# Two LoRA layers on one core: earlier loads of x and of layer 1's rows, and three slots instead of two for transposed x

## The reference, cut to what matters

```python
# layer 0 (adapters 6..15 of 32 are named by the ids), layer 1 (3..7 of 8)
x = x + (einsum('bsd,od->bso', x, base_weight) + base_bias
         + einsum('bsr,bor->bso', einsum('bsd,brd->bsr', x, lora_A_w[ids0]), lora_B_w[ids0]))
x = x + einsum('bnr,bor->bno', einsum('bni,bri->bnr', x, B[ids1]), A[ids1])   # SCALING is 1
```

## Time and profile before

| | us |
|---|---|
| median of 3 runs | 98.22 (97.95 to 98.42) |
| the profiled execution | 97.92 |
| its span, first to last instruction | 95.8 |
| PE busy | 91.5 (96%) |
| DVE, ACT, POOL busy | 64.8, 58.7, 58.0 |

### The profile page before, as it was taken

How to read it: one execution, slowest core, us unless ns; L and a number is a source line. 1 busy time by engine, 2 the same in 40 slices (tenths; PEclk the granted TensorE clock), 3 DMA queues, 4 the chain that set the end, 5 groups by cost and what they waited for, 6 DMA issues and landing times.

```text
span 95.8 us, 2305 instructions
## 1 busy us (share of the span) xinstructions
PE 91.5 (96%) x662; PEld 90.0 (94%) x662; DVE 64.8 (68%) x120; ACT 58.7 (61%) x189; POOL 58.0 (61%) x126
## 2 busy tenths in 40 slices
PE   5999999999999999999999999999999999999980
PEld 5899999999899998999999999999999999999970
DVE  4499799227076468959587877768595868786460
ACT  0074598874588796748494948567584949480210
POOL 6504008850568999999576584959585766808500
PEclk9999999999999999999999999999999999999998
DMA  2999998968896289989996499992836354520205
GB/s 40 312 347 387 374 403 262 281 156 214 215 224 223 53 250 238 310 249 235 203 290 218 70 319 209 238 269 91 228 44 229 34 213 54 200 110 0 110 0 219
DMA packets 16335, 19.45 MB, mean 203 GB/s; under 512 B 1444, under 2 KB 11556, under 8 KB 16164
## 3 DMA queue, kind: packets, MB, share of 16 engines
q1 hardware_dynamic: 15040, 14.04, 50.1%
q0 software_dynamic: 1280, 5.28, 22.1%
q10 hardware_dynamic: 4, 0.00, 0.0%
HBM read 13.47 MB, written 5.84 MB: 202 GB/s over the span
## 4 chain that ended last, share of the span: by engine, by line
PE 90%; DVE 4%; ACT 2%; issue 1%; DVEq 0%; ACTq 0%
PE psum L394 55%; PE psum L440 11%; PE psum L432 4%; PE psum L362 4%; PE psum L480 4%; PE psum L378 4%; PE psum L370 3%; DVE table_rounded L640 3%; PE psum L466 2%; PE psum L414 1%; PE psum L405 1%; PE psum L448 1%; DVE y L679 1%; ACT row_ends L558 1%; ACT table_rounded L558 1%
## 5 line engine op out<-in xcount | busy, mean ns | idle before, releaser
L394 PE MATMUL psum<-wd,xt 128*128 128x256 f32 (+1 forms) x384 | 62.3, 310 | 0.0
L394 PEld LDWEIGHTS psum<-wd,xt 128*128 128x128 f32 x384 | 56.1, 188 | 0.0
L558 ACT ACTIVATE wd<-table_rounded 128x128 fp32r x128 | 27.7, 297 | 14.7 <-PE psum L394 12.5
L339 POOL TENSOR_TENSOR up_rows<-gathered_rows,up_rows 128x512 fp32r<-128x512 f32 x16 | 20.6, 1289 | 14.0 <-ACT up_rows L558 14.0
L322 POOL DMA_INDIRECT gathered_rows<-by_rank,rows x16 | 15.9, 996 | 6.3 <-DMA by_rank<-row_ends 3.8
L640 DVE TENSOR_TENSOR xt<-psum,xt 128x512 fp32r<-128x512 f32 x16 | 11.1, 691 | 6.6 <-ACT xt L558 5.9
L647 DVE STREAM_TRANSPOSE psum<-x_squares 128x512 f32<-128x512 f32 x13 | 14.4, 1110 | 0.0
L440 PE MATMUL psum<-up_rows,u_sel 128*128 128x256 f32 x96 | 14.2, 284 | 0.0
L440 PEld LDWEIGHTS psum<-up_rows,u_sel 128*128 128x128 f32 x96 | 12.8, 190 | 0.2
L659 DVE STREAM_TRANSPOSE psum<-psum 128x128 f32<-128x128 f32 x16 | 5.3, 330 | 11.2 <-PE psum L394 7.8
L332 POOL TENSOR_TENSOR g_sel<-gathered_rows,batch_mask 128x16 f32<-128x16 f32 x64 | 12.1, 227 | 0.9 <-DMA gathered_rows<-by_rank,rows 0.7
(11 more groups left out here) (60 smaller groups left out, 72.1 us busy)
## 6 DMA issues: line engine op xcount, KB each, us to landing
out<-y SPq DMA_DIRECT2D x15, 256.0 KB
x_squares<-in_x SPq DMA_DIRECT2D x8, 256.0 KB
w_rows<-in_L_cond_base_weight SPq DMA_DIRECT2D x4, 256.0 KB, 4.0
bw_rows<-in_L_cond_lora_B_w SPq DMA_DIRECT2D x1, 1024.0 KB, 7.0
a_rows<-in_L_cond_lora_A_w SPq DMA_DIRECT2D x1, 1024.0 KB, 9.2
by_rank<-bw_by_rank SPq DMA_DIRECT2D x4, 256.0 KB
x_squares<-in_x SPq DMA_DIRECT2D x8, 128.0 KB
x_rows<-in_x SPq DMA_DIRECT2D x3, 256.0 KB, 9.3
```

The lines of the kernel that those rows point to most:

```text
L339: nc.gpsimd.tensor_tensor(out=up_rows[:, k % 2, LO, :], in0=gathered_rows[:, k % GATHERS, 0:D], in1=up_rows[:, k % 2, HI, :], op=ALU.subtr ...
L394: last = nc.tensor.matmul(bank_of(k, half)[:, start:end], xt[:, k % 2, c, x_part, :], wd[:, w_part, c, col:col + end - start], start=(c == ...
L558: return nc.scalar.activation(dst, src, ACT.Copy)
```

## The change

SP loads x's blocks 1 and 2 and layer 1's rows (`a1_rows`) before lora_A (`a_rows`), which goes to the end of the loads. `xt` gets three slots, so the transpose of block 2 moves ahead of `g` on PE, its copies move forward on ACT and DVE, and the left half of `base(2)` stands ahead of the second half of `base(0)`; that half is computed in one piece with D's columns, and `down` is gone. One of six warm-up matmuls and the two fillers behind `w0` are gone. ACT instead of DVE drains `b1`; a copy of one column (`table_call`) now stands first in ACT's list, and the register loads of the ids stand behind `w0`. In `select` the register load stands ahead of the wait. SP waits for the first gather before it issues the loads for blocks 4 and 5. On DVE and ACT the order around block 0's `own_u`, `u_high` and `up_high` is another.

```diff
-WARM_UPS = 6
-FILLERS = 2
+X_SLOTS = 3
+WARM_UPS = 5
@@ drains
-        ACT_DRAINS = ["w0", "w1", "w2", "w3", "c1", "g", "a0", "a1", "a2", "a3"]
-        DVE_DRAINS = ["b1", "w0", "w1", "w2", "w3", "bw0", "bw1", "bw2", "bw3", "c1", "a0", "a1", "a2", "a3"]
+        ACT_DRAINS = ["b1", "w0", "w1", "w2", "w3", "c1", "g", "a0", "a1", "a2", "a3"]
+        DVE_DRAINS = ["w0", "w1", "w2", "w3", "bw0", "bw1", "bw2", "bw3", "c1", "a0", "a1", "a2", "a3"]
@@ SP
             sp.dma_start(bw_rows[:, :, :], lora_b.rearrange("n (c p) r -> (n c) p r", p=P)).then_inc(bw_in, 16)
-            sp.dma_start(a_rows[:, :, :], lora_a.rearrange("(g n) r d -> (n r) g d", g=C)).then_inc(a_in, 16)
             load_x(1)
+            load_x(2)
             sp.wait_ge(a1_zeroed, 1)
             sp.dma_start(a1_rows[bass.ds(0, N1 * C, step=P // (N1 * C)), :, :],
                          l1_a.rearrange("n (c p) r -> (n c) p r", p=P)).then_inc(a1_in, 16)
-            load_x(2)
...
+            sp.dma_start(a_rows[:, :, :], lora_a.rearrange("(g n) r d -> (n r) g d", g=C)).then_inc(a_in, 16)
...
             for k in range(NBLK - 1):
+                if k == 0:
+
+                    sp.wait_ge(gathered[0], 16)
                 if k in (0, 1, 3, 6):
                     load_x(4 + (0, 1, 3, 6).index(k))
@@ PE
             w_fill(0)
-            keep_warm(FILLERS)
             wait_drained(pe, "b1")
...
             base(0, range(C), halves=[0])
+            x_fill(2)
...
             base(1, range(C), halves=[1])
-            x_fill(2)
+            wait_x(2)
+            wait_drained(pe, "a0")
+            base(2, range(C), halves=[0])
+
+
             wait_drained(pe, "c1")
-            base(0, [0, 1], halves=[1], with_d=False, group_check=False)
             wait_d(0)
-            down(0, [0, 1])
-            base(0, [2, 3], halves=[1], group_check=False)
+            base(0, range(C), halves=[1])
             wait_drained(pe, "a3")
             wait_d(1)
             base(1, range(C), halves=[0])
 
 
-            wait_x(2)
-            base(2, range(C), halves=[0])
             add_gh(0)
@@ ACT
+            act.wait_ge(warm_ready, 1)
+            copy(table_call[:, :], warm[:, 0:1])
+            wait_filled(act, "b1")
+            copy(b1_cols[:, :, :], chunked(fill_of("b1"))).then_inc(act_drained, 1)
+            w_high(0)
             act.wait_ge(ids_in, 32)
...
             select(1, L0, first[1, L0])
-            xt_high(2)
             select(2, L0)
+            up_high(0)
             select(2, L1)
-            up_high(0)
+            u_high(0)
             xt_high(3)
-            u_high(0)
@@ DVE
-            for q in range(4):
+            def lay_bw(q):
...
+            for q in range(3):
+                lay_bw(q)
+            xt_low(1)
+            lay_bw(3)
...
-            xt_low(1)
...
+            xt_low(2)
...
             turn_u(0)
-            xt_low(2)
+            own_u(0)
             x_turn(3)
-            own_u(0)
+            u_low(0)
             xt_low(3)
-            u_low(0)
```

More of the change, by code:

```diff
@@ L90, in two_lora_layers @@
         gathered_rows = sb("gathered_rows", [P, GATHERS, ROW])
-        xt = sb("xt", [P, 2, C, 2, P], F32R)
+        xt = sb("xt", [P, X_SLOTS, C, 2, P], F32R)
         up_rows = sb("up_rows", [P, 2, 2, D], F32R)
@@ L96, in two_lora_layers @@
         warm = sb("warm", [P, P])
+        table_call = sb("table_call", [P, 1])
         y = sb("y", [P, SLOTS, D])
@@ L381, in c1_part, with base @@
                     last.then_inc(filled, 1)
-            def base(k, chunks, with_d=True, halves=range(2), group_check=True):
+            def base(k, chunks, halves=range(2)):
                 left = W_LEFT[k % 2]
                 regions = [(left, left + HALF, P), (left, left + HALF, P + HALF)]
[L386 to L389, removed]
+                at_half, at = U_AT[k % 2]
+                start = min(at, left)
+                regions[at_half] = (start, start + HALF + P, min(D_AT[k % 2], P + at_half * HALF))
                 for c in chunks:
@@ L393, in base @@
                             start, end, col = regions[half]
-                            last = nc.tensor.matmul(bank_of(k, half)[:, start:end], xt[:, k % 2, c, x_part, :],
+                            last = nc.tensor.matmul(bank_of(k, half)[:, start:end], xt[:, k % X_SLOTS, c, x_part, :],
                                                     wd[:, w_part, c, col:col + end - start],
-                                                    start=(c == 0 and n == 0), stop=(c == C - 1 and n == 2),
-                                                    skip_group_check=not group_check)
-                if with_d and C - 1 in chunks and U_AT[k % 2][0] in halves:
+                                                    start=(c == 0 and n == 0), stop=(c == C - 1 and n == 2))
+                if C - 1 in chunks and U_AT[k % 2][0] in halves:
                     last.then_inc(u_filled, 1)
[L401 to L407, removed]
             def x_fill(k):
@@ L561, in xt_high, with select @@
                 act.wait_ge(xt_filled, k + 1)
+                if k >= X_SLOTS:
+                    act.wait_ge(u_filled, k - X_SLOTS + 1)
+                copy(xt[:, k % X_SLOTS, :, HI, :], chunked(XT)).then_inc(xt_hi_ready, 1)
+            def select(k, layer, n=None):
+                ready, table = ((sel0_ready, table0_rounded), (sel1_ready, table1_rounded))[layer]
+                n = n or adapters_of(act, k, layer)
                 if k >= 2:
                     act.wait_ge(u_filled, k - 1)
[L564 to L570, removed]
                 for b in range(NB):
@@ L591, in w_high @@
                 copy(w_columns(HI, oc), chunked(fill_of(f"w{oc}"))).then_inc(act_drained, 1)
+            act.wait_ge(warm_ready, 1)
[3 more added lines that the diff above has]
+            w_high(0)
             act.wait_ge(ids_in, 32)
             first = {(k, layer): adapters_of(act, k, layer) for k in range(2) for layer in (L0, L1)}
-            for oc in range(C):
+            for oc in range(1, C):
                 w_high(oc)
@@ L604, in _ @@
             copy(a1_by_rank[:, 0:R // 2, :], a1_rows[:, :, 0:R // 2].rearrange("p o r -> p r o")).then_inc(a1_by_rank_ready, 1)
+            xt_high(2)
             wait_drained(act, "c1")
@@ L652, in xt_low @@
                 dve.wait_ge(xt_hi_ready, k + 1)
-                low(xt[:, k % 2, :, LO, :], chunked(XT), xt[:, k % 2, :, HI, :]).then_inc(xt_lo_ready, 1)
+                low(xt[:, k % X_SLOTS, :, LO, :], chunked(XT), xt[:, k % X_SLOTS, :, HI, :]).then_inc(xt_lo_ready, 1)
             def turn_u(k):
@@ L703, in _ @@
             plus(0)
-            wait_filled(dve, "b1")
-            nc.vector.tensor_copy(b1_cols[:, :, :], chunked(fill_of("b1"))).then_inc(dve_drained, 1)
             lay_chunks(0)
```

## The result

The changed kernel takes 101.59 us (101.33 to 101.76, 4 runs) against 98.32 (97.95 to 98.62, 4 runs) of the kernel before: ratio 1.0332, interval 1.0287 to 1.0376. The forecast was 97.9, range 97.2 to 98.6. The profiled execution took 101.47 us with a span of 99.4, 3.6 more than before's 95.8.

A forecast was written before the change was run, and what follows sets the result against it. PE's list was taken to bound the kernel, with the gather and POOL setting `add_gh(2)`. Profiled 97.92 - 0.35 (gather sooner) = 97.57; with the median 0.30 above the profiled execution, 97.87, so 97.9 us; range 97.2 to 98.6.

The forecast's parts named there:

- The step that failed: Table's front part: stores unchanged in number and place, lora_A landing ahead of its use; costed at 0.
- Rival C: Opening: PE's thinner activity lets its clock rise later; priced at 1.4 us slower in sum, 99.6 us; chance 13%.
- The kernel's time is therefore the moment of `add_gh(2)` plus a constant: From `add_gh(2)`, at 36.16 before, PE's list to the end is the same in both kernels; forecast moment 35.8.
- `g` at about 16.0: Front part: `g` on PE waits for XT's copies and the last `bw_cols` copy, so starts where it stood, 16.04.
- PE at `x_fill(1)`: PE's opening: 0.65 us earlier, at 13.4, by fewer fillers and block 1 of x no longer behind lora_A.
- The 24 matmuls of 384 columns at 4.2: PE ahead of `add_gh(0)`: second half of `base(0)` starts at 24.55, then 24 matmuls at 0.174 us each.
- ready for `add_gh(0)` at 29.5, not 28.8: PE's list up to `add_gh(0)`: 1.1 us shorter, ready at 28.8 instead of 29.92, idle unless the gather lands sooner.
- The gather's own gain of 0.35: POOL's first `g_select` starts 0.35 us sooner, as loads for blocks 4 and 5 wait for gather 0.
- Rival B: Gather 0: the loads did not hold it, or others take their place; `add_gh(2)` at 36.16, 98.2 us; chance 17%.
- Rival A: Front part: `g` starts at 15.8 to 15.9, table up to 0.2 us earlier; gain 0.6, 97.6 us; chance 20%.

The follow-up runs named there:

- experiment 3: Changed kernel with lora_A's load between layer 1's rows and the two loads of the ids: 98.17 us, ratio 0.9942 to the kernel before.
- experiment 6: Changed kernel with the loads' tail in the order layer 1's rows, bias, lora_A, ids: 98.05 us, ratio 0.996 to the kernel before.
- experiment 1: Changed kernel with lora_A's load back in its old place, ahead of x1: 98.81 us, ratio 1.0023 to the kernel before.
- experiment 2: Kernel before with only SP's loads reordered as in the changed kernel: 100.55 us, ratio 1.0135.
- the ids-ahead kernel: Also experiment 5: changed kernel with lora_A's load between the ids and the bias, bias last: 100.61 us, ratio 1.0212 to the kernel before.
- experiment 7: Kernel of experiment 3 without SP's wait for gather 0: 98.10 us, ratio 0.9962 to the kernel before.
- experiment 4: Changed kernel with 11 matmuls on zeros filling PE's wait before `add_gh(0)`: 100.72 us, ratio 1.0177 to the kernel before.
- experiment 8: Kernel of experiment 3 with block 2's transposes behind `g`, copies moved with them, `bw3`'s copy ahead of `xt_low(1)`: 97.85 us, ratio 0.9914 to the kernel before.
- experiment 11: Kernel of experiment 8 with the order bias, lora_A, ids at the end of the loads: 97.52 us, ratio 0.9891 to the kernel before.
- experiment 12: Kernel of experiment 6 with the sixth warm-up matmul and the two fillers put back: 98.21 us, ratio 0.9933 to the kernel before.
- experiment 9: Changed kernel, lora_A still last, with the two loads of the ids issued from ACT's queue instead of SP's: 100.04 us, ratio 1.0106 to the kernel before.
- experiment 10: Kernel before with the two loads of the ids ahead of x's block 0, a single execution: 100.32 us.

## Why the prediction was wrong, point by point

**The step that failed** is this one: "The stores that carry the table, their number and place, do not change, and lora_A lands behind the other loads but ahead of its use behind `g`". The second half held: lora_A landed at 18.8, and its transposes began at 19.89. But the step priced the reordering by what arrives for its own user, and cost it at nothing. It moved the ids from behind lora_A to ahead of it. There the loads in 256-byte packets took the DMA engines to a share of 0.41 for three microseconds with a megabyte waiting, and the table's stores, behind that megabyte, landed late. Size: 2.66 us at the gather. Undoing it brings the gather back to 25.21 and 24.51 (experiments 3 and 6) and the time back in experiments 1, 3 and 6; doing it alone makes the gather 2.07 late (experiment 2). Of the 2.66, 0.40 were at the store already (0.28 of it since ACT's copy of `g` began at 20.09, not 19.81); the other 2.26 are more than the 1.8 of the missing bytes, and what makes up that rest stays open.

Why did it cost so little before? The ids stood behind every large load but the bias, so the hole fell at 14.5 to 16 us, and what followed were the bias and the stores; it may still have cost some tenths, for with the ids last the gather goes 0.70 earlier than in experiment 3. The row of transfers of the kernel before, 11 to 17 us, has its dip there, shorter and less deep; why it is smaller there is not shown:

```profile
DMA  9999999999999989889899986554666899999999
```

**The second loss, 1.3 us, is the clock.** Stretches of the changed kernel; the number before the share is the clock:

```profile
32.00:33.00 1.00, 0.79 (x3) 0.79 (x4) 0.59 (x1) 0.59 (x4) 1.00 (x2) 0.63 0.90 234
33.00:34.00 1.00, 1.00 (x4) 1.00 (x4) 0.52 (x2) 1.00 (x4) 0.85 (x2) 0.50 0.96 287
34.00:35.00 1.00, 1.00 (x6) 1.00 (x5) 0.96 (x3) 1.00 (x5) 0.98 (x5) 0.50 1.14 213
```

Behind the wait of 2.71 us PE ran at 0.50, the 1.2 GHz level, until between 35 and 36. Rival C was about the clock too, but it looked at the start of the kernel, not at a wait that another error would open. All four runs of the changed kernel had a mean clock of 0.983; the ids-ahead kernel had it in one of four with a wait as long. What decides between them stays open. So the 3.6 us of the spans are 2.66 (gather issued) - 0.31 (issue to first `g_select`, 4.33 before and 4.02 now) - 0.06 (from there to `add_gh(0)`, 0.96 and 0.90) + 1.28 (7.55 for 6.27), which gives 3.57.

**What held.** "The kernel's time is therefore the moment of `add_gh(2)` plus a constant": 3.57 at that moment, 3.6 in the span. `g` at about 16.0: it came at 16.24, a little outside the 0.1 that the prediction allowed itself, its last copy (`bw_cols`) at 15.41 to 16.09 instead of the 16.05 reckoned:

```profile
15.41 0.68 DVE L718 COPY bw_cols<-psum 128x512 f32<-128x512 f32 x1
```

PE at `x_fill(1)`: 13.4 forecast, 13.49 measured. The 24 matmuls of 384 columns at 4.2: measured 4.47, ready for `add_gh(0)` at 29.5, not 28.8, since they began at 25.03 and not 24.55; PE's list was shorter by 0.4, not 1.1, and all of it was idle time, as argued. The gather's own gain of 0.35 (bounds 0 and 0.66): 0.40 between experiments 3 and 7. From issue to the first `g_select` the profiles with SP's wait have 3.99 to 4.17 us (nine of them, and 5.29 in experiment 4), those without it 4.33 to 4.41 (three). Experiment 2 has 4.01 without the wait; its gather goes at 26.70, when SP has issued all the squares (by 25.60). The changed kernel's goes later still, so its 0.31 cannot be put down to the wait. Rival B ("the loads were not what held the gather") has most of the traces against it, though for the time it was as good as right: without the wait the kernel is no slower. By the Trainium skill, page "DMA: Bandwidth & Descriptors", section "Queues, rings and completion order", as the prediction has it with B, queues take turns. That does not exclude the gain: sharing also delays. Rival A, that `g` moves, may have something behind it: experiments 8 and 11 made `g` 1.02 and 0.84 us earlier than in the kernel before and are the two fastest, but their lead over experiments 3 and 6 is not clear of noise.

In hindsight a number in front of the reader pointed to it: in the earlier trace rows x's loads took up to 9.4 us to land, so a queue this deep sets what the order in it costs, and the ids' loads stand between lora_A's old place and its new one. A row of the DMA engines' share around 14 to 16 us of the kernel before (0.83 and 0.74 with 276 and 239 GB/s, where 12 to 14 has 416 and 400) would have shown what they do.

**What stays open** is why 256 packets of 256 bytes keep 16 engines largely idle for about 3 us. By the Trainium skill, page "DMA: Bandwidth & Descriptors", section "Specifications", a transfer below 512 bytes doesn't reach the line rate because it becomes a read-modify-write. The traces agree in part: the 2 KB broadcast of the bias left no hole in experiment 6 and a short one in 11 and 12, the 256-byte ones a long one. The packets' own time does not explain it: at 15 ns each (experiment 9) all 256 fill the 16 engines for 0.24 us. Where the rest of the 3 us goes, and whether the short packets, the one source row read 128 times, or both do it, was not tried.

## What to carry to other kernels

When a large load changes its place in a queue, look at what small transfers it lets pass, not only at when it lands itself: loads of a few hundred bytes per partition belong behind the last large one, and the DMA share of each microsecond shows their hole while all engines look busy. Price an opened wait of PE with what its clock may lose behind it, here 1.3 us on a wait of 2.7. And follow a store's landing to who waits for it: from the last store's issue to the gather it was 5.7 to 6.4 us where the ids stood ahead of lora_A in SP's queue (experiments 2, 4, 5 and the changed kernel), and 4.0 to 4.9 where they stood behind it. It does not show a hole that lies earlier: experiments 9 and 10 have 3.8 and 3.9, and their loss is in the opening.

## What the runs showed of the hardware that was not expected

- 64 KB of broadcast ids took the 16 DMA engines down to shares of 0.06 to 0.55 for about 3 us, on either issuing engine's queue. With large loads behind them `g` or the gather came 2.1 to 2.7 us late, and the time rose by 1.1 to 3.3 us. Their own packets took 15 ns each.
- Behind a wait of PE of 2.71 us, and in experiment 2 of 1.99, the granted clock fell to the 1.2 GHz level and cost 1.2 to 1.3 us (7.55 and 7.47 us from `add_gh(0)` to `add_gh(2)`, for 6.27 to 6.31); behind one of 2.63 us in another kernel's profile it did not.
- Ids that are last leave no hole: in experiments 6, 11 and 12 they move between 14.5 and 16.3 us, among the table's stores, with the DMA engines at a share of 1.05 to 1.10.
